# Gate and leftover ahead of U's low part on VectorE, zero rows in the packed image, one power for GpSimd's root

## The reference, cut to what matters

```python
x = x + conv(gn(x))                       # 192 + 28 channels -> 192
t = tokens(x)                             # 8 images x 256 tokens x 192
t = t + attn(ln(t), wq, wk, wv)           # softmax(q k^T / sqrt(192), causal) v
gate = ln(t) @ Wg.T + bg                  # 8 experts, the largest is taken
t = t + W3[e] @ (silu(W1[e] @ ln(t)) * (W2[e] @ ln(t)))
```

## Time and profile before

| | us |
|---|---|
| median of 3 runs | 257.18 (256.59 to 257.24) |
| profiled execution | 255.9 |
| its span | 254.1 |
| TensorE busy in the span | 204.0 |
| VectorE busy | 170.7 |
| ScalarE busy | 115.7 |
| GpSimd busy | 106.3 |
| granted TensorE clock, mean | 0.912 of full speed |

### The profile page before, as it was taken

One profiled execution on the slowest core, in us unless ns is written; L12 is line 12 of the kernel. 1 busy time (PEld: TensorE's weight loads), 2 busy tenths in 40 slices (PEclk: granted clock), 3 DMA queues, 4 the chain that ended last, 5 costly groups with the idle time before them and its releaser, 6 DMA issues.

```text
span 254.1 us, 4807 instructions
## 1 busy us (share of the span) xinstructions
PE 204.0 (80%) x1342; PEld 182.7 (72%) x1342; DVE 170.7 (67%) x559; ACT 115.7 (46%) x235; POOL 106.3 (42%) x124
## 2 busy tenths in 40 slices
PE   0496799999769999898672118999999999999970
PEld 0495798888668779777562106999999999999960
DVE  2576788564555889777878723687777876877641
ACT  2366465343658878775752001433434334334320
POOL 3154423520295589888988700113223132132231
PEclk9999599999979999999775555999999999999996
DMA  6991632357006056446520212233210000000000
GB/s 206 373 287 40 198 114 71 100 171 330 3 0 215 3 213 239 99 173 232 174 102 4 76 49 66 52 98 86 76 50 18 16 24 4 31 33 3 31 11 0
DMA packets 15734, 25.86 MB, mean 102 GB/s; under 512 B 3767, under 2 KB 12659, under 8 KB 14688
## 3 DMA queue, kind: packets, MB, share of 16 engines
q1 hardware_dynamic: 13840, 22.40, 27.1%
q0 software_dynamic: 1872, 3.18, 3.6%
HBM read 19.50 MB, written 6.76 MB: 103 GB/s over the span
## 4 chain that ended last, share of the span: by engine, by line
PE 55%; DMA 13%; DVE 11%; issue 7%; ACT 6%; POOL 5%; POOLq 1%; SPq 1%; DVEq 0%; ACTq 0%
PE bank L1248 6%; DMA stage<-in_w_all 5%; PE bank L985 4%; PE bank L988 4%; PE bank L987 4%; PE bank L986 4%; PE bank L989 4%; PE bank L1224 4%; DMA out_rows<-yo,rows 3%; DMA xcm<-in_x_cm 3%; PE bank L1249 3%; PE bank L1239 2%; POOL token_rows L406 2%; PE bank L1094 1%; PE bank L1028 1%
## 5 line engine op out<-in xcount | busy, mean ns | idle before, releaser
L452 POOL DMA_INDIRECT out_rows<-yo,rows x23 | 22.4, 973 | 82.0 <-DVE yo L952 73.9
L1248 PE MATMUL bank<-wall,HH 128*128 x92 | 29.4, 374 | 1.5 <-DVE HL L932 1.5
L937 DVE TENSOR_TENSOR gh<-gh,bank 128x470 f32<-128x470 f32 x23 | 14.8, 645 | 22.1 <-PE bank L989 20.5
L608 ACT ACTIVATE HH<-bank 128x512 fp32r<-128x512 f32 x23 | 13.8, 599 | 27.4 <-PE bank L1224 27.4
L614 ACT ACTIVATE FH<-bank 128x256 fp32r<-128x256 f32 x23 | 8.9, 385 | 33.9 <-PE bank L1239 31.8
L1249 PE MATMUL bank<-wall,HL 128*128 x92 | 23.1, 252 | 0.0
L406 POOL DMA_INDIRECT token_rows<-rows,posi x16 | 18.8, 1177 | 7.7 <-issue 7.4
L424 POOL TENSOR_TENSOR wall<-stage,wall 128x940 fp32r<-128x940 f32 x8 | 18.6, 2328 | 5.6 <-ACT wall L505 3.0
L985 PE MATMUL bank<-wall,FH 128*128 x46 | 19.8, 430 | 1.1 <-DVE FL L940 1.0
L611 ACT ACTIVATE gh<-bank 128x470 f32<-128x470 f32 x23 | 13.0, 565 | 13.6 <-PE bank L989 13.6
L1248 PEld LDWEIGHTS bank<-wall,HH 128*128 128x128 f32 x92 | 17.3, 188 | 1.8 <-issue 1.7
(11 more groups left out here) (217 smaller groups left out, 658.3 us busy)
## 6 DMA issues: line engine op xcount, KB each, us to landing
stage<-in_w_all SPq DMA_DIRECT2D x8, 1324.0 KB, 6.3
rows<-token_rows SPq DMA_DIRECT2D x23, 98.0 KB
near_rows<-gram SPq DMA_DIRECT2D x8, 243.0 KB, 2.8
xcm<-in_x_cm SPq DMA_DIRECT2D x2, 768.0 KB, 8.5
rows<-in_x_tm SPq DMA_DIRECT2D x1, 1536.0 KB, 14.1
token_rows<-emptyt SPq DMA_DIRECT2D x1, 882.0 KB, 5.2
taps_sb<-near_rows SPq DMA_DIRECT2D x8, 103.0 KB, 2.0
small_sb<-in_small SPq DMA_DIRECT2D x1, 704.0 KB, 8.4
```

The lines of the kernel that those rows point to most:

```text
L452: pool.indirect_dma_start(out=out, out_offset=bass.IndirectOffsetOnAxis(ap=rows[:, j, C + 2:C + 3].bitcast(U32), axis=0), in_=yo[:, par], ...
L1248: nc.tensor.matmul(dst[:, 0:2 * C], HH[:, 1 - par, k], w(0, P, c0, c0 + 2 * C), start=(k == 0), stop=False)
```

## The change

On VectorE the gate and the leftover come directly behind the attention output, ahead of U's low part and of the rows' statistics. The statistics are written straight into the rows' last columns, and VectorE adds the epsilon there (one instruction more). GpSimd's `token_root` is one power in that column, where it was an addition, a power and a copy. The second part of the image is turned once and not twice, its low rows are written below its high rows by a second instruction in `low_xt`, and the low parts of U, of the projection and of the values' weights have tiles of their own (`uBl`, `mBl`, `vwBl`), 64 rows of which are set to zero once at the start. Two identity products fill a part of bank 0 once. `project`, `values` and `scores` take the same number of matmuls of the same shapes as before.

```diff
@@ -410,11 +411,8 @@
             def token_root(b):
 
                 pool.wait_ge(var_ready, b + 1 + AHEAD)
-                nc.gpsimd.tensor_scalar(lnv[:], ln2[:, :, 1], EPS, None, ALU.add).then_inc(ln_ready, 1)
-                pool.wait_ge(ln_ready, b + 1)
-                nc.gpsimd.tensor_tensor(ln2[:, :, 1], lnv[:], half_c[:, 0:HALVES], ALU.pow).then_inc(rs_ready, 1)
-                pool.wait_ge(rs_ready, b + 1 + AHEAD)
-                nc.gpsimd.tensor_copy(rows[:, HALVES * b:HALVES * (b + 1), C:C + 2], ln2[:]).then_inc(t2_ready, 1)
+                y = rows[:, HALVES * b:HALVES * (b + 1), C + 1]
+                nc.gpsimd.tensor_tensor(y, y, half_c[:, 0:HALVES], ALU.pow).then_inc(t2_ready, 1)
 
             def weights_lo(e):
 
...
@@ -735,14 +735,14 @@
             def low_xt(t, par):
 
                 ve.wait_ge(xh_ready, t + 1 + AHEAD)
-                nc.vector.tensor_tensor(XL[:, par].rearrange("p t x -> p (t x)"), bank[0][:],
-                                        XH[:, par].rearrange("p t x -> p (t x)").bitcast(F32), ALU.subtract).then_inc(xl_ready, 1)
+                nc.vector.tensor_tensor(XL[:, par], bank[0][:, 0:PIX], XH[:, par, 0].bitcast(F32), ALU.subtract)
+                nc.vector.tensor_tensor(XH[CB:P, par, 1], bank[0][0:CB, PIX:2 * PIX], XH[0:CB, par, 1].bitcast(F32), ALU.subtract).then_inc(xl_ready, 1)
 
             def low_u(t, par):
 
                 ve.wait_ge(uh_ready, t + 1 + AHEAD)
                 nc.vector.tensor_tensor(uAl[:, par], bank[1][:, 0:PIX], UH[:, par, 0].bitcast(F32), ALU.subtract)
-                nc.vector.tensor_tensor(UH[CB:P, par, 1], bank[1][CB:P, PIX:2 * PIX], UH[CB:P, par, 1].bitcast(F32), ALU.subtract).then_inc(ul_ready, 1)
+                nc.vector.tensor_tensor(uBl[0:CB, par], bank[1][0:CB, PIX:2 * PIX], UH[0:CB, par, 1].bitcast(F32), ALU.subtract).then_inc(ul_ready, 1)
 
             def leftover(e):
 
...
@@ -780,18 +780,6 @@
                         ins = nc.vector.scalar_tensor_tensor(out=row, in0=bank[5][:, C * h:C * (h + 1)], scalar=rsum[:, h:h + 1], in1=row,
                                                              op0=ALU.mult, op1=ALU.add)
                     ins.then_inc(o_taken, 1)
-                    ve.wait_ge(o_taken, t - 1 + AHEAD)
-                    hold()
-                    for h in range(HALVES):
-                        ins = nc.vector.bn_stats(tstat[:, h], rows[:, bass.ds(2 * t + (h - 4), 1), 0:C].rearrange("p a c -> p (a c)"))
-                    link(ins)
-                    ve.wait_ge(t2_ready, t - 2 + AHEAD)
-                    hold()
-                    for h in range(HALVES):
-                        ins = nc.vector.bn_aggr(ln2[:, h], tstat[:, h])
-                    ins.then_inc(var_ready, 1)
-                if on(t, 0):
-                    low_u(t, par)
                 if on(t, 3):
 
                     ve.wait_ge(g_ready, t - 2 + AHEAD)
...
@@ -807,6 +795,22 @@
                     link(nc.vector.tensor_tensor(lg[:], lg[:], desc, ALU.mult))
                     link(nc.vector.tensor_reduce(gmx[:], lg[:], AX_X, ALU.max))
                     nc.vector.tensor_tensor(oh[:], lg[:], gmx[:].rearrange("p (h a) -> p h a", a=1).to_broadcast(wide), ALU.is_equal).then_inc(oh_ready, 1)
+                if 0 <= t - 2 < EXPERTS:
+                    leftover(t - 2)
+                if on(t, 0):
+                    low_u(t, par)
+                if on(t, 2):
+
+                    ve.wait_ge(o_taken, t - 1 + AHEAD)
+                    hold()
+                    for h in range(HALVES):
+                        ins = nc.vector.bn_stats(tstat[:, h], rows[:, bass.ds(2 * t + (h - 4), 1), 0:C].rearrange("p a c -> p (a c)"))
+                    link(ins)
+                    for h in range(HALVES):
+                        ins = nc.vector.bn_aggr(rows[:, 2 * t + (h - 4), C:C + 2], tstat[:, h])
+                    link(ins)
+                    y = rows[:, 2 * t - 4:2 * t - 2, C + 1]
+                    nc.vector.tensor_scalar(y, y, EPS, None, ALU.add).then_inc(var_ready, 1)
                 if on(t, 3):
 
                     ve.wait_ge(pf_ready, t - 2 + AHEAD)
...
@@ -817,8 +821,6 @@
                     link(nc.vector.tensor_reduce(pos[:], lg[:], AX_X, ALU.add))
                     hold()
                     nc.vector.tensor_copy(posi[:, bass.ds(2 * t - 6, 2)], pos[:]).then_inc(pos_ready, 1)
-                if 0 <= t - 2 < EXPERTS:
-                    leftover(t - 2)
                 if done[0] < LINKS:
                     ve.sem_inc(dve2, LINKS - done[0])
                 assert done[0] <= LINKS
...
@@ -1069,10 +1072,10 @@
                     c = slice(CA * m, CA * (m + 1))
                     q = slice(2 * CA + CA * m, 2 * CA + CA * (m + 1))
                     nc.tensor.matmul(dst, mH[:, c], XH[:, par, 0], start=True, stop=False)
-                    nc.tensor.matmul(dst, mH[:, c], XL[:, par, 0], start=False, stop=False)
+                    nc.tensor.matmul(dst, mH[:, c], XL[:, par], start=False, stop=False)
                     nc.tensor.matmul(dst, mL[:, c], XH[:, par, 0], start=False, stop=False)
                     nc.tensor.matmul(dst, mH[:, q], XH[:, par, 1], start=False, stop=False)
-                    mm = nc.tensor.matmul(dst, mH[:, q], XL[:, par, 1], start=False, stop=True)
+                    mm = nc.tensor.matmul(dst, mBl[:, c], XH[:, par, 1], start=False, stop=True)
                 mm.then_inc(u_ready, 1)
 
             def values(t, par):
...
@@ -1090,8 +1097,7 @@
                 pe.wait_ge(xl_ready, t + 1 + AHEAD)
                 for h in range(HALVES):
                     nc.tensor.transpose(bank[0][:, P * h:P * (h + 1)], xn[:, h, 0:CA], ident)
-                    for p0 in (0, CB):
-                        mm = nc.tensor.matmul(bank[0][p0:p0 + CB, PIX + P * h:PIX + P * (h + 1)], xn[:, h, CA:C], ident, start=True, stop=True)
+                    mm = nc.tensor.transpose(bank[0][0:CB, PIX + P * h:PIX + P * (h + 1)], xn[:, h, CA:C], ident)
                 mm.then_inc(xt_ready, 1)
 
             def turn_rows(t):
...
@@ -1192,6 +1199,8 @@
 
                     pe.wait_ge(small2_in, 16)
                     pe.wait_ge(gvar_ready, len(GANGS))
+                    nc.tensor.matmul(bank[0][:, PIX:PIX + P], ident, ident, start=True, stop=True)
+                    nc.tensor.matmul(bank[0][:, PIX + P:2 * PIX], ident, ident, start=True, stop=True)
                     wg, ones = c2("wg"), c2("tri")[:, P:2 * P]
                     nc.tensor.matmul(bank[0][:, 0:EXPERTS], ones, wg[:, 0:EXPERTS], start=True, stop=False)
                     nc.tensor.matmul(bank[0][:, 0:EXPERTS], ones, wg[:, EXPERTS:2 * EXPERTS], start=False, stop=True).then_inc(gate_sum, 1)
```

More of the change, by code:

```diff
@@ L129, in build @@
         vwL = sb("vwL", [P, C], F32R)
+        mBl = sb("mBl", [P, 2 * CA], F32R)
+        vwBl = sb("vwBl", [P, C], F32R)
         tri_sb = sb("tri_sb", [P, 2 * P], BF16)
@@ L178, in build @@
         XH = sb("XH", [P, 2, 2, PIX], F32R, middle)
-        XL = sb("XL", [P, 2, 2, PIX], F32R, middle)
+        XL = sb("XL", [P, 2, PIX], F32R, middle)
         UH = sb("UH", [P, 2, 2, PIX], F32R, middle)
         uAl = sb("uAl", [P, 2, PIX], F32R, middle)
+        uBl = sb("uBl", [P, 2, PIX], F32R, middle)
         V = sb("V", [P, 2, HALVES, C], ctx=middle)
@@ L186, in build @@
         ln1v = sb("ln1v", [P, TILES], ctx=middle)
-        ln2 = sb("ln2", [P, HALVES, 2], ctx=middle)
-        lnv = sb("lnv", [P, HALVES], ctx=middle)
         rsum = sb("rsum", [P, 2], ctx=middle)
@@ L243, in build @@
          exp_ready, pt_ready, pt_copied, o_ready, t2_ready, t2t_ready, x2_copied, g_ready, oh_ready, pf_ready,
-         pos_ready, var_ready, rs_ready, ln_ready, ln1_ready, o_taken, dve2, wall_hi, wall_lo) = (sem(n) for n in (
+         pos_ready, var_ready, ln1_ready, o_taken, dve2, wall_hi, wall_lo) = (sem(n) for n in (
              "xn_ready", "xt_ready", "xh_ready", "xl_ready", "u_ready", "uh_ready", "ul_ready", "v_ready", "v_copied",
              "s_ready", "max_ready", "exp_ready", "pt_ready", "pt_copied", "o_ready", "t2_ready", "t2t_ready",
-             "x2_copied", "g_ready", "oh_ready", "pf_ready", "pos_ready", "var_ready", "rs_ready", "ln_ready", "ln1_ready", "o_taken", "dve2", "wall_hi", "wall_lo"))
+             "x2_copied", "g_ready", "oh_ready", "pf_ready", "pos_ready", "var_ready", "ln1_ready", "o_taken", "dve2", "wall_hi", "wall_lo"))
         group_in, attn_in, attn_split = sem("group_in"), sem("attn_in"), sem("attn_split")
@@ L250, in build @@
         held, wall_q, wall_hi3 = sem("held"), sem("wall_q"), sem("wall_hi3")
-        gate_sum, gate_ready = sem("gate_sum"), sem("gate_ready")
+        gate_sum, gate_ready, zeroed = sem("gate_sum"), sem("gate_ready"), sem("zeroed")
         scattered, table_ready = sem("scattered"), sem("table_ready")
@@ L428, in weights_lo @@
                                         w3[:, :, 0].bitcast(F32), ALU.subtract).then_inc(wall_lo, 1)
-            for s in (rs_ready, t2_ready):
```

(25 more changed lines are left out.)

## The result

The changed kernel takes 267.41 us (median of 4 runs, 265.95 to 268.02), the kernel before 256.88 beside it (4 runs); the ratio is 1.0428, with a 95% interval of 1.0375 to 1.0482. The change costs 10.5 us. The profiled execution, 268.02 us with a span of 266.1, is the slowest of its four, so the spans differ by 12.0. Some medians in the table of the experiments hold disturbed runs (e5's above all), which the ratios leave out, and the profiled execution of e10 was one, so that no step is given for it.

A forecast was written before the change was run, and what follows sets the result against it. It took GpSimd to bound the middle stage, with VectorE as full. +16.4 for the ring and -0.3 for the rest gave +16.1 on the profiled 255.9, 272.0; with the median 1.3 higher, 273 us, range 264 to 278.

The forecast's parts named there:

- The collision: Middle stage: GpSimd's two weight subtractions (the pair) need 3.95 us, but VectorE's step leaves 2.99 us free of two-SBUF-operand instructions.
- The ring: Middle stage: pair, held VectorE gate, late statistics, root and scatters wait on each other, 12.1 us a step for 8.7.
- Two scatters with their gaps: Term of the ring: GpSimd's two indirect DMAs behind the power, with the idle time ahead of them, 3.03 us.
- End of the pair to the statistics: Term of the ring: VectorE's rest of the gate, leftover, U and statistics after the pair ends, 4.32 us.
- Step by step: Forecast starts of GpSimd's pair, expert by expert through the middle stage, reaching +15.3 us at expert 7.
- the dearer of the two cases: Steps 8 and 9: the pair goes ahead of VectorE's leftover, and the middle stage ends 17.6 us later.
- The middle of +16.4: End of the middle stage: taken between +17.6 us and +15.2 us, the latter if the leftover goes first.
- The likeliest case: Whole kernel: the main case, in which the ring holds, 269 to 276 us, chance 0.74.
- Two of the signs: Predicted trace marks: GpSimd's L422 11 to 12.5 us apart in steps 4 to 7; experts' first row 15 to 18 later.
- A turn at the seam: Rival: VectorE gets in between GpSimd's two subtractions, about +9 us, 266 us; chance 0.08.
- No hold: Rival: small VectorE instructions are not held by GpSimd's pair, -1.0 us, 256.2 us; chance 0.07.
- TensorE at its low clock: Rival: pauses drop TensorE to 1.2 GHz, its step of about 13 us becomes the ring, 277 us; chance 0.08.

The follow-up runs named there:

- e5: The changed kernel with the gate's small tile in PSUM and the leftover first in VectorE's step: 255.15 us, ratio 0.9873 to the kernel before.
- e10: The kernel of e9 with the gate's small tile in PSUM besides: 253.2 us, ratio 0.9865 to the kernel before.
- e2: The changed kernel with the gate's small tile in PSUM, order unchanged: 261.78 us, ratio 1.0204 to the kernel before.
- e3: The changed kernel with GpSimd's two weight subtractions replaced by five memsets, low parts of the weights zero: 251.29 us, ratio 0.9836 to the kernel before.
- e4: The kernel before with VectorE's new order alone, keeping the three-instruction root and the old image packing: 272.94 us, ratio 1.0652 to the kernel before.
- e6: The changed kernel with the statistics put back directly behind the attention output: 253.07 us, ratio 0.9894 to the kernel before.
- e7: The changed kernel with the leftover alone put back to the end of VectorE's step: 264.65 us, ratio 1.0309 to the kernel before.
- e9: The kernel of e6 with the addition of epsilon moved behind the gate's first two instructions: 253.49 us, ratio 0.988 to the kernel before.

## Why the prediction was right, and where its sizes were off

**The collision.** Right. "It needs 3.95 us and finds 2.99" is what the rows show, and e2 and e3 show the exclusion by operand from both sides. L794 took 3.6 us in steps 5 to 7 and 3.8 in 8 and 9, which lies in the 3 to 4 us forecast.

**The ring.** Right in its members, 1.2 us too long: 12.1 forecast, 10.92 measured. Two terms were mis-sized. *Two scatters with their gaps*, 3.03, are 2.52: I carried over the gap of 0.65 us that stands behind a copy, which the change takes out; e4, which keeps the copy and the longer root, has 12.0 us. *End of the pair to the statistics*, 4.32, is 3.62: the rest of the gate 0.70 and not 0.83 (a held L794 ends with the pair and does not start with it), U 0.67 and not 0.90, statistics with addition 1.08 and not 1.42 (the aggregation L810 starts 0.03 us behind L807, where the one before, L791, stood behind a wait for GpSimd's copy and started 0.18 us behind its L786, and the added link cost nothing that shows). The power (0.80 with its wait) and the pair were right, and so was the image's low part in two instructions (0.89 for 0.90). VectorE's own step was put at 8.3 us; e3, with the same instructions on VectorE, has steps of 7.7.

**Step by step.** L422 of experts 2 to 7 was forecast at 88.6, 101.2, 112.8, 124.9, 137.0 and 147.5; it came at 88.2, 99.4, 110.3, 121.2, 132.1 and 142.4. The error grows by 0.7 to 1.4 us a step up to 132.1 and then by 0.3, most of it as the ring says. The list has 11.6 us from 101.2 to 112.8 where its own ring has 12.1, and gives no reason. In steps 8 and 9 the pair went first, 0.21 us ahead of L794 in both, which was the dearer of the two cases: +17.6 by the forecast terms, +12.0 in fact. VectorE had waited for TensorE 0.53 and 1.12 us there, which the forecast did not have. The middle of +16.4 lies nearer only because it mixes in the cheaper case.

**The rest.** The early stage was to give 0.3 us back; GpSimd's first pair starts at 70.52 and not at 70.98, 0.5 us. ScalarE's wait for the weight loads (8.0 us before) is gone. The forecast of 273 is 5.6 us above the median, inside the range. 4.0 of it lie between the sum and the profiled execution (272.0 and 268.02), most of it from the two terms; the rest comes from where the profiled executions lie, 1.3 below the median before and 0.6 above it after (and 273.3 was rounded to 273). The likeliest case's own range (269 to 276) was too high by 1.6 at its lower end. Two of the signs missed as well: L422 came 10.9 us apart in steps 5 to 7 and not 11 to 12.5, and the experts' rows 12.0 us later and not 15 to 18.

**The rivals.** *A turn at the seam* would have given 266 us, nearer to the median than my own number, and is refuted all the same: L794 was held across 112.43. Its nearness is chance. *No hold* is refuted. *TensorE at its low clock*: from 80 to 120 us it was granted the full clock, and the steps were 10.9 us long all the same. From 130 us it stood at 0.50. There VectorE waited for it, 0.53 us in step 8 and 1.12 in step 9, but L794 was held to the pair's end in both, and the step from 132.13 to 142.36 was 10.23 us, shorter than those before it by about U's 0.67. The windows of the changed kernel; the last three columns are the granted clock, the DMA share and GB/s, and ahead of them stand the busy times of TensorE, its weight loads, VectorE, ScalarE and GpSimd:

```profile
100.00:110.00 10.00, 6.96 (x59) 6.25 (x57) 9.47 (x26) 5.84 (x13) 5.80 (x5) 1.00 0.40 142
110.00:120.00 10.00, 6.70 (x55) 5.79 (x54) 9.39 (x25) 6.36 (x13) 6.02 (x5) 1.00 0.35 125
120.00:130.00 10.00, 6.87 (x48) 6.14 (x49) 9.32 (x27) 5.53 (x11) 5.86 (x5) 0.90 0.34 110
130.00:140.00 10.00, 6.14 (x27) 4.74 (x26) 9.03 (x25) 4.55 (x9) 6.49 (x5) 0.50 0.25 100
```

## What to carry to other kernels

When GpSimd works in long stretches on SBUF beside VectorE, look for the stretch of VectorE's step in which no instruction has two SBUF operands; it is a resource. Here an order that left no such stretch as long as GpSimd's cost 2.2 to 2.6 us a step. A small instruction with one operand can be held too, as the addition was. Before a block is taken ahead of another, follow who waits for the one that is pushed back: here it was the statistics, and putting them back alone was worth 14 us. Putting one operand in PSUM freed the comparison from the exclusion without moving it (e2: 0.18 us for 3.62), but the next instruction with two was then held in its place.

## What the runs showed of the hardware

- The exclusion reaches instructions of 16 numbers a row with two SBUF operands (3.8 us in the changed kernel, 4.68 in e4) and the addition of 2 numbers a row with one (0.64 us in e6, 2.57 in e9's step 9); it holds across two GpSimd instructions that follow each other (five times in the changed kernel). The addition is held by memsets as well (0.38 to 0.44 us in e3), the others are not.
- It also acts on GpSimd's indirect DMAs: 1.04 us alone, 1.99 us (e7) and 1.80 us (e9) beside a VectorE subtraction of 940 numbers a row that had begun within the 0.3 us before it. In e6 the subtraction begins 0.34 us behind the DMA's start, and the DMA takes 1.04.
- Behind a copy on GpSimd the next indirect DMA starts 0.65 us later (e4, before), behind a power 0.19 us later. Why was not tried.
- U's low part in two instructions takes 0.67 us in place of 0.90, with the same sizes, now that its second part is read from and written to rows 0 to 63 and not rows 64 to 127 (116.15 to 116.82; 91.72 to 92.62 in the earlier trace rows). Reading alone does not do it: the image's second part (L739) is read from rows 0 to 63 and written to rows 64 to 127, and the two instructions take 0.89 us. The timeline of VectorE in the changed kernel:

```profile
118.96 0.42 DVE L738 TENSOR_TENSOR XL<-bank,XH 128x256 fp32r<-128x256 f32 x1
119.40 0.42 DVE L739 TENSOR_TENSOR XH<-bank,XH 64x256 fp32r<-64x256 f32 x1
119.85 0.29 DVE L772 CUSTOM_DVE_ANT_0 rows<-bank,small_sb 128x128 f32<-128x128 f32 x1
```
